# Head of a graph-network kernel: order of the loads, number and pace of the early tiles

## The chip, the cores and the metric

One core of a Trainium2 chip runs the kernel. The metric is the device time of one execution in microseconds (us), as the median of several runs.

## The reference

The input is a graph: `x` with 3125 nodes of 128 features, and 53125 edges (`src`, `dst`, a relation `type` of 0 to 7), sorted by `dst`, 17 to a node on average. Cut to what matters:

```python
h = relu(layernorm(x))
for L in 0, 1, 2:                                  # RGCN, W: [8, 128, 128]
    out = h @ root[L] + b[L]
    for r in range(8):
        msg = where(type == r, (h @ W[L][r])[src], 0)
        cnt = segment_sum(type == r, dst)
        out += segment_sum(msg, dst) / max(cnt, 1)
    h = relu(out)
x = x + h
g = relu(layernorm(x))                             # GIN
z = relu((g + segment_sum(g[src], dst)) @ W1 + b1) @ W2 + b2
out = x + g + (z - mean(z)) * rsqrt(var(z) + eps) * gamma + beta
```

## The kernel before

**Tiles.** Edges lie in 416 tiles of 128; nodes in 25 blocks of 128, loaded and normalized in 7 groups of 4 blocks (the last has one). For each layer there is an h table in DRAM, with one row for each node and relation (`h @ W[r]`). For each tile GpSimd gathers 128 rows of that table by an indirect DMA (`gather`, L1034) into a ring of 32 slots, VectorE builds a 128 x 64 selection matrix with the weights 1/count (`select`, L796), and TensorE multiplies both and so sums the tile into its window of 64 nodes (`sum_tile`, L464). GpSimd waits on `s_mm`, which counts batches of eight summed tiles, before it overwrites a slot: behind the first table, gather n (from 0, n a multiple of 8 and at least 32) waits until tile n - 25 of the count is summed. Layer 3 (GIN) works with a dense adjacency and no gathers.

**The early tiles.** The first 40 tiles of layer 0 (`FORE`) don't use the h table. GpSimd gathers their rows from the table of normalized x (`x0_table`, L1041), which is ready sooner. VectorE's `fore_select` (L767, 128 x 512, a ring of 12) keeps node and relation apart, `fore_tile` (L482) sums them into "key banks" of 64 nodes x 8 relations, ScalarE copies a full bank to SBUF, and `key_bank` (L492) multiplies it by the eight weights into the first sum. `fore_tile` opens a bank with a multiplication by zeros (L478). TensorE does 12 early tiles and then, by `head_order`, one tile of the h table and one early tile by turns.

**The head in order.** SP loads x (L947), then small weights, and stores each normalized group as x0 (L953). ScalarE issues `dst`, `type`, `src`, the first layer's relation weights (w0), and four loads of `dst` shifted by one and by 64 edges (L1066 to L1069; the first of them has 127 rows and 206.9 KB). Then it normalizes the groups (L598), turns them (`scalar_xT`, L592) and evacuates the 50 half blocks of the first table that TensorE makes (`transform`, L438; `evacuate`, L614). The tables go through a ring of three stages (`STAGES`) and out by SP (`store_rows`, L912 and L914). VectorE waits for all five `dst` loads (`s_edges`, L1173), builds keys, and tests by the shifted edges whether the graph fits the windows. TensorE sums the test (`s_metric` to `s_total`, L1391), and VectorE sets `flag` (L1211). Each engine reads the flag and branches into the windowed path (taken here) or a general one. SP waits for the flag before the first table store, GpSimd before the first x0 gather.

**Counts.** The keys of the edges are written to DRAM (L970 to L974) and come back broadcast to all partitions in chunks of 16 tiles (`load_chunk`, L923, 1088 KB each, two buffers). VectorE matches each tile's keys against them (L775) to count. SP puts chunks 0 and 1 in front of the table stores, and chunks 2 and 3 behind the stores of tables 10 and 19 (`CHUNK_BEHIND`).

**The order of TensorE in the table stage** is: per group the transforms of its blocks, then the turn of a later group; the sum of the test stands behind group 0.

Of the kernel before, what the change touches and what calls it, by code (L numbers as in the profile page):

```python
# [5 lines left out]
ALU = mybir.AluOpType  # L6
# [49 lines left out]
FORE = 40  # L56
FORE_RING = 12
KEY_BANK = 64
# [16 lines left out]
def gnn_kernel(nc, x, src_t, dst_t, type_t, limits, w_rel, root_w, bias_w,  # L75
# [16 lines left out]
    SLACK = max(P * t // DEG - LEAD - start_of[t] for t in range(TILES))  # L92
# [50 lines left out]
    FORE_STEP = start_of[BATCH] - start_of[0]  # L143
    assert all(start_of[t] == FORE_STEP * (t // BATCH) + STEP * (t % BATCH) - LEAD for t in range(FORE))

    def key_pieces(t):

        s, found = start_of[t], []
# [6 lines left out]
    KEY_BANKS = cdiv(start_of[FORE - 1] + SPAN, KEY_BANK)  # L155
# [18 lines left out]
    with ExitStack() as ctx:  # L174
# [59 lines left out]
        key_turn = shared(4 * P).rearrange("p (q k) -> p q k", k=P)  # L234
# [4 lines left out]
        fore_at = shared(FORE).bitcast(I32)  # L239
        key_near = shared(FORE)  # L240
# [3 lines left out]
        fore_sel = early[:, taken[7]:taken[7] + FORE_RING * KEYS].rearrange("p (a k) -> p a k", k=KEYS)  # L244
        assert taken[8] - taken[7] == EARLY + NP and taken[9] - taken[7] >= FORE_RING * KEYS
# [11 lines left out]

        match = agg_s[:].rearrange("p a k -> p (a k)").bitcast(BF16).rearrange("p (a k) -> p a k", a=BATCH)
# [27 lines left out]
        s_edges = sem("s_edges")  # L286
        s_src = sem("s_src")
# [646 lines left out]
        CHUNK_BEHIND = {10: 2, 19: 3}  # L934
# [6 lines left out]
        def _(sp):  # L941
# [16 lines left out]
            for L in range(GIN):  # L958
                if L:
                    sp.dma_start(w_all[:, L, 0:REL, :], w_rel[L].rearrange("r f o -> f r o")).then_inc(s_w, 16)  # L960
                sp.dma_start(w_all[:, L, REL, :], root_w[L]).then_inc(s_w, 16)
                sp.dma_start(vecs[:, L:L + 1], bias_w[L].rearrange("(p o) -> p o", o=1)).then_inc(s_w, 16)
                store_x0(L)
            sp.dma_start(w_gin[:, 0, :], gin_w1).then_inc(s_w, 16)
            sp.dma_start(w_gin[:, 1, :], gin_w2).then_inc(s_w, 16)
            for n, v in enumerate((gin_b1, gin_b2, gamma, beta)):
                sp.dma_start(vecs[:, 3 + n:4 + n], v.rearrange("(p o) -> p o", o=1)).then_inc(s_w, 16)
# [7 lines left out]
            for g in range(GIN, GROUPS):  # L975
                store_x0(g)
            sp.wait_ge(s_key_out, 48)
            load_chunk(sp, 0)
            load_chunk(sp, 1)
            sp.wait_ge(s_flag, 1)  # L980
            fast = sp.value_load(flag[0:1, 0:1], min_val=0, max_val=1)
            with sp.If(fast != 0):
# [12 lines left out]
                for b in range(BLOCKS):  # L995
                    if turn_of(0, b, 1) >= CHUNK * (CHUNKS - 3):
                        store_rows(sp, 1, b)
                for b in range(BLOCKS):
                    store_rows(sp, 2, b)
            with sp.Else():  # L1000
                for b in range(BLOCKS):
                    store_rows(sp, 0, b)
                for c in range(2, CHUNKS):
# [16 lines left out]
        def _(pool):  # L1020
# [6 lines left out]
            nc.gpsimd.iota(iota_i, pattern=[[1, EARLY + NP]], base=-EARLY, channel_multiplier=0).then_inc(s_pool_const, 1)  # L1027
            pool.wait_ge(s_idx, 1)
# [8 lines left out]
            with pool.If(fast != 0):  # L1037
                pool.wait_ge(s_src, 32)
                pool.wait_ge(s_x0, 16 * GROUPS)
                for t in range(FORE):  # L1040
                    pool.indirect_dma_start(fore_rows[:, t, :], None, x0_table,  # L1041
                                            bass.IndirectOffsetOnAxis(ap=src_i[:, t:t + 1], axis=0)
                                            ).then_inc(s_fore_row[t // BATCH], 16)
# [17 lines left out]
        def _(act):  # L1061
# [24 lines left out]
            scalar_norm(act, GROUPS - 1)  # L1086
            for g in range(GROUPS):
# [8 lines left out]
            act.wait_ge(s_w, 16 * (2 * GIN + 2 + 6))  # L1096
# [66 lines left out]
        def _(dve):  # L1163
# [8 lines left out]
            dve.wait_ge(s_edges, 80)  # L1172
            nc.vector.tensor_scalar(dst_pad, dst_i3[:], 0.0, float(PAD_NODE + 1), ALU.is_lt, ALU.mult  # L1173
# [4 lines left out]
            nc.vector.tensor_tensor(dst_f3[:], dst_i3[:], dst_pad, ALU.add).then_inc(s_edge_f, 1)  # L1178
# [8 lines left out]
            dst, after, far = (dst_f3[:, n, 0:TILES] for n in range(3))  # L1187
            nc.vector.tensor_tensor(broke[:, 0, :], after, dst, ALU.is_lt)
# [23 lines left out]
            dve.wait_ge(s_iota, 1)  # L1212
            dve.wait_ge(s_flag, 1)
            fast = dve.value_load(flag[0:1, 0:1], min_val=0, max_val=1)
            with dve.If(fast != 0):
# [11 lines left out]
                match_to(BATCH)  # L1227
# [4 lines left out]
                for t in range(FORE, HEAD + SELS - BATCH, BATCH):  # L1232
# [3 lines left out]
                    for f in range(FORE_RING + t - FORE, min(FORE_RING + t - FORE + BATCH, FORE)):  # L1236
                        fore_select(dve, f)
# [60 lines left out]
            with dve.Else():  # L1298
                nc.vector.memset(norm[:], 0.0).then_inc(g_found, 1)
# [66 lines left out]
        def _(pe):  # L1366
# [26 lines left out]
            pe.wait_ge(s_w, 16 * (2 * GIN + 2 + 6))  # L1393
# [139 lines left out]
```

## Time and profile before

| | us |
|---|---|
| median of 3 runs | 1685.67 |
| lowest, highest | 1683.42, 1686.53 |
| profiled execution | 1682.43 |
| its span, first to last instruction | 1680.6 |

| engine | busy us | share of the span |
|---|---|---|
| GpSimd (POOL) | 1186.0 | 71% |
| TensorE (PE) | 1170.9 | 70% |
| VectorE (DVE) | 868.2 | 52% |
| ScalarE (ACT) | 645.3 | 38% |

Busy shares are means over stages with different limits. In the rows, SPq, ACTq and POOLq are the instructions by which an engine issues DMAs, and a name behind "<-" in brackets is what ended the idle time before the row. Line numbers are those of the kernel.

### The profile page before, as it was taken

Reading aid. Unit: us, or ns where it says so; the run is one execution under the profiler, and the core shown is the slowest. Engines: PE = TensorE matmul, PEld = TensorE weight load, DVE = VectorE, ACT = ScalarE, POOL = GpSimd, SP = SyncE. Lnnn points to the kernel's source line nnn. Section 1 sums busy time; section 2 is a strip of 40 time slices with the busy share of each in tenths; the row PEclk is TensorE's granted clock in tenths of the full one; section 3 lists DMA queues with packets and bytes.
Section 4 is the critical chain, followed back from the end, with each engine's and each line's share of the span. In section 5 each row is a group of like instructions: output and inputs, shape, how many; then the busy total and the mean of one; then the engine's idle time right before and its main releaser. Section 6 shows DMA issues by size and latency. Waiting matters only on the chain.

```text
span 1680.6 us, 17006 instructions
## 1 busy us (share of the span) xinstructions
PE 1170.9 (70%) x4448; PEld 775.0 (46%) x4448; DVE 868.2 (52%) x3241; ACT 645.3 (38%) x1137; POOL 1186.0 (71%) x1256
## 2 busy tenths in 40 slices
PE   3799565657566777777777878765667666666777
PEld 1357444435344544444454545544545454544543
DVE  4647855455555177787778777751222222222213
ACT  4520500000000278888888888860011111212224
POOL 0757777777777577777777777757777777777770
PEclk9899755555555555758575756575567776768898
DMA  6963544353533311323232323231111111111111
GB/s 169 314 231 106 184 130 134 123 162 100 164 116 93 100 54 54 96 60 97 59 98 59 98 59 97 67 98 52 53 52 53 52 54 52 53 52 53 53 53 40
DMA packets 81154, 159.35 MB, mean 95 GB/s; under 512 B 24337, under 2 KB 38556, under 8 KB 77724
## 3 DMA queue, kind: packets, MB, share of 16 engines
q0 software_dynamic: 39936, 81.87, 18.4%
q1 hardware_dynamic: 39354, 74.73, 12.5%
q10 hardware_dynamic: 1762, 1.59, 0.4%
q8 instruction: 39, 0.64, 0.2%
q14 instruction: 63, 0.52, 0.1%
HBM read 115.33 MB, written 42.77 MB: 94 GB/s over the span
## 4 chain that ended last, share of the span: by engine, by line
POOL 67%; issue 22%; PE 5%; DMA 3%; ACT 1%; ACTq 1%; DVE 1%; SPq 0%; POOLq 0%; DVEq 0%
POOL rows L1034 67%; PE ps_h L438 3%; DMA h_table<-stage 2%; DMA rows<-h_table,idx 1%; PE ps_agg L464 1%; DMA early<-in_dst_t 1%; ACTq L1067 1%; ACT early L598 0%; PE ps_agg L1483 0%; ACT stage L614 0%; PE ps_h L558 0%; PE ps_agg L541 0%; PE ps_a L558 0%; PE ps_a L564 0%; PE ps_h L529 0%
## 5 line engine op out<-in xcount | busy, mean ns | idle before, releaser
L1034 POOL DMA_INDIRECT rows<-h_table,idx x1208 | 1143.5, 947 | 398.5 <-issue 367.2
L464 PE MATMUL ps_agg<-sel,rows 128*128 128x64 f32 (+12 forms) x2786 | 718.8, 375 | 443.5 <-DMA rows<-h_table,idx 433.1
L464 PEld LDWEIGHTS ps_agg<-sel,rows 128*128 128x128 f32 x2786 | 605.3, 278 | 737.8 <-DMA rows<-h_table,idx 586.3
L796 DVE TENSOR_SCALAR sel<-iota,early,norm 128x64 f32<-128x64 f32 x1208 | 358.0, 329 | 435.4 <-PE ps_agg L464 433.6
L891 DVE TENSOR_TENSOR early<-ps_a,early 128x300 f32 x416 | 197.8, 475 | 126.2 <-PE ps_a L509 115.4
L702 ACT ACTIVATE scratch<-scratch,ones 128x300 bf16<-128x300 f32 x416 | 223.2, 536 | 50.4 <-PE ps_a L509 42.6
L708 ACT ACTIVATE scratch<-iota,code_lo 128x300 f32<-128x300 f32 x416 | 226.4, 545 | 12.5
L438 PE MATMUL ps_h<-w_all,xT 128*128 128x512 f32 x300 | 197.8, 772 | 16.7 <-ACT stage L614 16.7
L775 DVE TENSOR_SCALAR_CACHE_REDUCE agg_s<-scratch,key_f 128x256 bf16<-128x256 f32 x416 | 194.2, 472 | 27.1 <-DMA scratch<-key_rows 16.7
L509 PE MATMUL ps_a<-scratch 128*128 128x300 bf16 x416 | 169.7, 409 | 0.9 <-DVE early L891 0.9
L880 DVE TENSOR_SCALAR scratch<-iota,code_lo 128x128 bf16<-128x128 f32 x416 | 145.1, 349 | 0.0
L614 ACT COPY stage<-ps_h 128x512 f32<-128x512 f32 x100 | 57.6, 585 | 197.3 <-PE ps_h L438 176.1
L674 ACT CAST stage<-early 128x3072 bf16<-128x3072 uint8 x13 | 35.7, 2751 | 175.9 <-PE ps_a L529 172.7
L619 ACT ACTIVATE xT<-ps_agg,vecs 128x512 f32<-128x512 f32 (+2 forms) x16 | 9.4, 587 | 229.7 <-PE ps_agg L464 229.7
L509 PEld LDWEIGHTS ps_a<-scratch 128*128 128x128 bf16 x416 | 96.4, 232 | 1.8 <-issue 1.7
L438 PEld LDWEIGHTS ps_h<-w_all,xT 128*128 128x128 f32 x300 | 63.1, 243 | 45.4 <-ACT stage L614 22.5
L614 DVE COPY stage<-ps_h 128x512 f32<-128x512 f32 x50 | 34.1, 683 | 90.8 <-PE ps_h L438 90.8
L1041 POOL DMA_INDIRECT early<-x_table,early x40 | 38.2, 956 | 51.1 <-issue 51.1
L674 ACT CAST w_all<-early 128x3072 bf16<-128x3072 uint8 x12 | 32.9, 2751 | 74.4 <-PE ps_a L529 74.4
L626 ACT ACTIVATE hid<-ps_agg,vecs 128x512 f32<-128x512 f32 (+3 forms) x10 | 5.3, 526 | 135.3 <-PE ps_agg L464 135.3
L447 PE MATMUL ps_agg<-xT,w_all 128*128 128x512 f32 (+3 forms) x52 | 36.6, 801 | 10.7 <-issue 6.1
L482 PE MATMUL ps_a<-early 128*128 128x464 f32 (+29 forms) x150 | 42.1, 410 | 0.0
(128 smaller groups left out, 546.0 us busy)
## 6 DMA issues: line engine op xcount, KB each, us to landing
h_table<-stage SPq DMA_DIRECT2D x150, 256.0 KB, 2.5
scratch<-key_rows SPq DMA_DIRECT2D x26, 1088.0 KB, 6.1
rows<-h_table,idx POOLq DMA_INDIRECT x1208, 2.5
x_rows<-in_x SPq DMA_DIRECT2D x6, 256.0 KB, 7.1
x_table<-early SPq DMA_DIRECT2D x6, 256.0 KB, 3.0
out<-early SPq DMA_DIRECT2D x6, 256.0 KB
w_all<-in_W SPq DMA_DIRECT2D x2, 512.0 KB, 4.2
early<-x_table,early POOLq DMA_INDIRECT x40, 4.0
```

The source lines that it names most:

```text
L438: nc.tensor.matmul(half_bank(L, b, half)[:], xT[:, block_of(b)], w_all[:, L, 4 * half:4 * half + 4, :].rearrange("p r o -> p (r o)"), star ...
L464: mm = nc.tensor.matmul(sums_of(L, k)[:, at:at + width], rows[:, G % SLOTS, :], sel[:, G % SELS, in_window:in_window + width], start=False ...
L509: nc.tensor.matmul(ps_a[a % A_BANKS][:, 0:HOT], low[:, a % HOTS, :], hot[:, a % HOTS, :], start=True, stop=True).then_inc(s_step, 1)
L614: copy(stage[:, H % STAGES, 512 * half:512 * half + 512], half_bank(L, b, half)[:]).then_inc((s_evA, s_evD)[half], 1)
L674: nc.scalar.copy(fill_of(b), adjacency[:, b, 0:SPARE]).then_inc(s_fill, 1)
L702: nc.scalar.activation(hot[:, a % HOTS, :], apart[:, a % 2, :], ACT.Relu, bias=ones[:, 0:1], scale=-1.0).then_inc(s_hot, 1)
L708: nc.scalar.activation(apart[:, a % 2, :], iota[:, EARLY:EARLY + HOT], ACT.Abs, bias=code[:, a:a + 1]).then_inc(s_apart, 1)
L775: done = nc.vector.tensor_scalar(match[:, t % BATCH, :], chunks[:, c % 2, at:at + 2 * P], key_f[:, t:t + 1], 0.0, ALU.is_equal, ALU.add, a ...
L796: done = nc.vector.tensor_scalar(mine, here, dst, norm[:, t:t + 1], ALU.is_equal, ALU.mult)
L880: nc.vector.tensor_scalar(low[:, a % HOTS, :], iota[:, EARLY:EARLY + P], lo_f[:, a:a + 1], None, ALU.is_equal).then_inc(s_low, 1)
L891: nc.vector.tensor_tensor(mine, ps_a[a % A_BANKS][:, 0:HOT].rearrange("p (b d) -> p b d", d=REACH), mine, ALU.add).then_inc(s_add, 1)
L1034: pool.indirect_dma_start(rows[:, slot, :], None, table, bass.IndirectOffsetOnAxis(ap=column, axis=0)).then_inc(landed, 16)
```

## The change

SP: w0 is loaded behind x instead of by ScalarE; x0 stores 0 to 4 come before the key store; root weights, biases and the other small loads (14) go two at a time behind the stores of tables 0 to 6. These seven tables are stored before SP waits for the flag. The relation weights of layers 1 and 2 (`load_w`) are loaded behind the last table store. Chunks 2 and 3 stand behind tables 13 and 20.

ScalarE: `dst`, `type` and `src` are loaded first, and the four shifted loads are issued behind all norms and the first `scalar_xT`, in front of the table's evacuations.

VectorE: pads and converts only the unshifted `dst` at first, and the shifted ones behind all groups of x, when it also waits for them (`s_shifted`). TensorE sums the test behind group 1.

GpSimd: the x0 gathers stand in front of the wait for the flag. `FORE` is 48, and the head has two early tiles to each later tile (`FORE_PACE`), so that it ends at tile 66 instead of 68. The early windows have their own starts (`fore_start`). Some buffers lie elsewhere.

```diff
-FORE = 40
+FORE = 48
 FORE_RING = 12
+FORE_PACE = 2
...
-    for t in range(FORE_RING, FORE):
-        head_order += [("tile", FORE + t - FORE_RING), ("fore", t)]
-    HEAD = 2 * FORE - FORE_RING
+    for t in range(FORE_RING, FORE, FORE_PACE):
+        head_order += [("tile", FORE + (t - FORE_RING) // FORE_PACE)] + [("fore", f) for f in range(t, t + FORE_PACE)]
+    HEAD = FORE + (FORE - FORE_RING) // FORE_PACE
...
+                    if b == 0 and L == 1:
+                        pe.wait_ge(s_wr, 16 * (GIN - 1))
...
-        CHUNK_BEHIND = {10: 2, 19: 3}
+        SP_BRANCH = 7
+        CHUNK_BEHIND = {13: 2, 20: 3}
...
-            for L in range(GIN):
-                if L:
-                    sp.dma_start(w_all[:, L, 0:REL, :], w_rel[L].rearrange("r f o -> f r o")).then_inc(s_w, 16)
...
+            sp.dma_start(w_all[:, 0, 0:REL, :], w_rel[0].rearrange("r f o -> f r o")).then_inc(s_w0, 16)
+            for g in range(5):
+                store_x0(g)
...
+            for b in range(SP_BRANCH):
+                store_rows(sp, 0, b)
+                for into, what in small_loads[2 * b:2 * b + 2]:
+                    sp.dma_start(into, what).then_inc(s_w, 16)
...
             sp.wait_ge(s_flag, 1)
...
-                for b in range(BLOCKS):
+                for b in range(SP_BRANCH, BLOCKS):
                     store_rows(sp, 0, b)
...
+                load_w()
...
+            pool.wait_ge(s_src, 32)
+            pool.wait_ge(s_x0, 16 * GROUPS)
+            for t in range(FORE):
+                pool.indirect_dma_start(fore_rows[:, t, :], None, x0_table,
+                                        bass.IndirectOffsetOnAxis(ap=src_i[:, t:t + 1], axis=0)
+                                        ).then_inc(s_fore_row[t // BATCH], 16)
             pool.wait_ge(s_idx, 1)
             pool.wait_ge(s_flag, 1)
...
-            act.dma_start(w_all[:, 0, 0:REL, :], w_rel[0].rearrange("r f o -> f r o")).then_inc(s_w0, 16)
-            act.dma_start(dst_i3[0:P - 1, 1, :], dst_t[1:P, 0:COLS]).then_inc(s_edges, 16)
...
             scalar_norm(act, GROUPS - 1)
+            scalar_xT(act, 0)
+            act.dma_start(dst_i3[0:P - 1, 1, :], dst_t[1:P, 0:COLS]).then_inc(s_shifted, 16)
+            act.dma_start(dst_i3[0:HALO, 2, :], dst_t[HALO:P, 0:COLS]).then_inc(s_shifted, 16)
+            act.dma_start(dst_i3[HALO:P, 2, :], dst_t[0:HALO, 1:COLS + 1]).then_inc(s_shifted, 16)
+            act.dma_start(dst_i3[P - 1:P, 1, :], dst_t[0:1, 1:COLS + 1]).then_inc(s_shifted, 16)
...
-            dve.wait_ge(s_edges, 80)
...
+            dve.wait_ge(s_edges, 16)
...
             norm_x(dve, GROUPS - 1)
...
+            dve.wait_ge(s_shifted, 64)
+            nc.vector.tensor_scalar(dst_pad[:, 1:3, :], dst_i3[:, 1:3, :], 0.0, float(PAD_NODE + 1), ALU.is_lt, ALU.mult
+                                    ).then_inc(s_edge_f, 1)
...
                 table0(g)
-                if g == 0:
+                if g == 1:
                     pe.wait_ge(s_metric, 1)
```

## Rows read from the trace of the kernel before

**Rows 1.** Page: chain that ended last by engine and line; costliest group

```profile
POOL 67%; issue 22%; PE 5%; DMA 3%; ACT 1%; ACTq 1%; DVE 1%; SPq 0%; POOLq 0%; DVEq 0%
...
L1034 POOL DMA_INDIRECT rows<-h_table,idx x1208 | 1143.5, 947 | 398.5 <-issue 367.2
```

**Rows 2.** Waits of GpSimd: who it waited for, us in total, times, longest

```profile
POOL rows L1034 <- issue: 367.2, 1205, 0.3
...
POOL rows L1034 <- DMA h_table<-stage: 31.3, 3, 11.8
```

**Rows 3.** Timeline, GpSimd: start us, us, line, operation, out<-in, count [idle before]

```profile
45.02 1.11 POOL L1041 DMA_INDIRECT early<-x_table,early  x1 [39.26 <-issue]
...
94.20 0.94 POOL L1041 DMA_INDIRECT early<-x_table,early  x1 [0.30 <-issue]
104.80 0.94 POOL L1034 DMA_INDIRECT rows<-h_table,idx  x1 [9.65 <-DMA h_table<-stage]
```

**Rows 4.** Timeline, TensorE in the head

```profile
104.81 3.12 PE L482 MATMUL ps_a<-early 128*128 128x296 f32 x8
...
123.46 0.33 PE L464 MATMUL ps_agg<-sel,rows 128*128 128x64 f32 x2
123.63 1.08 PE L482 MATMUL ps_a<-early 128*128 128x280 f32 x4
124.55 0.33 PE L464 MATMUL ps_agg<-sel,rows 128*128 128x64 f32 x2
...
158.88 5.89 PE L492 MATMUL ps_agg<-hid,w_all 128*128 128x64 f32 x48
164.59 2.58 PE L464 MATMUL ps_agg<-sel,rows 128*128 128x30 f32 x22
```

**Rows 5.** Timeline, all engines, 0 to 44

```profile
3.58 8.92 ACTq L1067 DMA_DIRECT2D early<-in_dst_t  x1
4.73 0.87 DVE L746 BATCH_NORM_STATS2 ln_stat<-x_rows 128x6 f32<-128x128 f32 x4 [2.97 <-DMA x_rows<-in_x]
...
23.31 0.81 DVE L1173 TENSOR_SCALAR rows<-early 128x1251 f32<-128x1251 int32 x1 [7.57 <-DMA early<-in_dst_t]
...
34.86 2.02 ACT L598 ACTIVATE early<-x_rows,ln_nm,ln_rs 128x128 f32<-128x128 f32 x5
...
35.27 0.59 DVE L1188 TENSOR_TENSOR rows<-early 128x416 f32<-128x416 f32 x1
...
37.25 1.54 ACT L614 COPY stage<-ps_h 128x512 f32<-128x512 f32 x3
...
37.91 1.26 SPq L923 DMA_DIRECT2D scratch<-key_rows  x2
...
43.03 0.16 DVE L1211 TENSOR_SCALAR flag<-ps_a 128x1 int32<-128x1 f32 x1 [0.60 <-PE ps_a L1391]
```

**Rows 6.** DMA issues: count, KB each, median us to landing (where known)

```profile
early<-in_src_t ACTq DMA_DIRECT2D x1, 208.5 KB, 5.2
...
early<-in_dst_t ACTq DMA_DIRECT2D x1, 206.9 KB
```

**Rows 7.** Windows: stretch, length, busy by engine, TensorE's clock, DMA share, GB/s

```profile
12.50:23.30 10.80, 1.08 (x4) 0.71 (x4) 0.34 (x2) 3.42 (x7) 0.00 (x0) 1.00 0.42 115
37.90:104.80 66.90, 52.66 (x117) 22.77 (x118) 36.21 (x147) 32.72 (x55) 38.24 (x41) 0.85 0.91 313
110.00:115.00 5.00, 5.00 (x24) 3.77 (x23) 4.02 (x14) 0.00 (x0) 3.78 (x5) 1.00 0.19 52
...
110.00:165.00 55.00, 55.00 (x313) 43.00 (x311) 43.19 (x174) 3.51 (x6) 41.90 (x44) 1.00 0.37 114
```

**Rows 8.** Timeline, SP's queue: store of table 7

```profile
58.23 0.32 SPq L912 DMA_DIRECT2D h_table<-stage  x1
```

**Rows 9.** Timeline, VectorE in the head: early selects

```profile
118.29 2.78 DVE L767 TENSOR_SCALAR early<-iota,early,norm 128x512 f32<-128x512 f32 x6
```

More of the change, by code:

```diff
@@ L91, in gnn_kernel @@
     start_of = [P * (t - t % BATCH) // DEG - LEAD + STEP * (t % BATCH) for t in range(TILES)]
-    SLACK = max(P * t // DEG - LEAD - start_of[t] for t in range(TILES))
+    FORE_STEP = start_of[BATCH] - start_of[0]
+    fore_start = [FORE_STEP * (t // BATCH) + STEP * (t % BATCH) - LEAD for t in range(FORE)]
+    assert all(fore_start[t] <= start_of[t] for t in range(FORE))
+    SLACK = max(P * t // DEG - LEAD - s for t, s in [*enumerate(start_of), *enumerate(fore_start)])
     assert all(P * t // DEG - LEAD >= start_of[t] >= -EARLY for t in range(TILES)) and SLACK < LEAD
@@ L142, in gnn_kernel @@
     assert FORE % BATCH == 0
-    FORE_STEP = start_of[BATCH] - start_of[0]
-    assert all(start_of[t] == FORE_STEP * (t // BATCH) + STEP * (t % BATCH) - LEAD for t in range(FORE))
     def key_pieces(t):
-        s, found = start_of[t], []
+        s, found = fore_start[t], []
         for j in range(KEY_BANKS):
@@ L153, in key_pieces @@
         return found
-    KEY_BANKS = cdiv(start_of[FORE - 1] + SPAN, KEY_BANK)
+    KEY_BANKS = cdiv(fore_start[FORE - 1] + SPAN, KEY_BANK)
     key_tiles = [[t for t in range(FORE) if any(p[0] == j for p in key_pieces(t))] for j in range(KEY_BANKS)]
@@ L238, in gnn_kernel @@
         fore_rows = shared(FORE * D).rearrange("p (a f) -> p a f", f=D)
-        fore_at = shared(FORE).bitcast(I32)
-        key_near = shared(FORE)
+        fore_at = rest[:, 0:FORE].bitcast(I32)
+        key_near = rest[:, FORE:2 * FORE]
         assert taken[-1] <= OWN + BLOCKS * NA // 4
@@ L243, in gnn_kernel @@
         KEYS = REL * KEY_BANK
-        fore_sel = early[:, taken[7]:taken[7] + FORE_RING * KEYS].rearrange("p (a k) -> p a k", k=KEYS)
-        assert taken[8] - taken[7] == EARLY + NP and taken[9] - taken[7] >= FORE_RING * KEYS
+        fore_sel = early[:, taken[6]:taken[6] + FORE_RING * KEYS].rearrange("p (a k) -> p a k", k=KEYS)
+        assert taken[7] - taken[6] == EARLY + NP and taken[8] - taken[6] >= FORE_RING * KEYS
         y_rows = xr_rows
@@ L256, in gnn_kernel @@
         base_i = key_f[:, 0:TILES].bitcast(I32)
+        key_turn = agg_s[:, 0, :].rearrange("p (q k) -> p q k", k=P)
         match = agg_s[:].rearrange("p a k -> p (a k)").bitcast(BF16).rearrange("p (a k) -> p a k", a=BATCH)
@@ L286, in gnn_kernel @@
         s_edges = sem("s_edges")
+        s_shifted = sem("s_shifted")
+        s_wr = sem("s_wr")
         s_src = sem("s_src")
@@ L957, in _ @@
                 load_x(g)
-            for L in range(GIN):
-                if L:
-                    sp.dma_start(w_all[:, L, 0:REL, :], w_rel[L].rearrange("r f o -> f r o")).then_inc(s_w, 16)
[L961 to L967, printed above, removed]
+            sp.dma_start(w_all[:, 0, 0:REL, :], w_rel[0].rearrange("r f o -> f r o")).then_inc(s_w0, 16)
+            for g in range(5):
+                store_x0(g)
             whole = COLS // P
@@ L974, in _ @@
             sp.dma_start(key_rows[0:1, 0:HALO], halo[:]).then_inc(s_key_out, 16)
-            for g in range(GIN, GROUPS):
+            for g in range(5, GROUPS):
                 store_x0(g)
@@ L979, in _, with load_w @@
             load_chunk(sp, 1)
+            small_loads = [(w_all[:, L, REL, :], root_w[L]) for L in range(GIN)]
+            small_loads += [(vecs[:, L:L + 1], bias_w[L].rearrange("(p o) -> p o", o=1)) for L in range(GIN)]
+            small_loads += [(w_gin[:, 0, :], gin_w1), (w_gin[:, 1, :], gin_w2)]
+            small_loads += [(vecs[:, 3 + n:4 + n], v.rearrange("(p o) -> p o", o=1))
+                            for n, v in enumerate((gin_b1, gin_b2, gamma, beta))]
+            for b in range(SP_BRANCH):
+                store_rows(sp, 0, b)
+                for into, what in small_loads[2 * b:2 * b + 2]:
+                    sp.dma_start(into, what).then_inc(s_w, 16)
+            assert 2 * SP_BRANCH >= len(small_loads)
             sp.wait_ge(s_flag, 1)
             fast = sp.value_load(flag[0:1, 0:1], min_val=0, max_val=1)
+            def load_w():
+                for L in range(1, GIN):
+                    sp.dma_start(w_all[:, L, 0:REL, :], w_rel[L].rearrange("r f o -> f r o")).then_inc(s_wr, 16)
             with sp.If(fast != 0):
-                for b in range(BLOCKS):
+                for b in range(SP_BRANCH, BLOCKS):
                     store_rows(sp, 0, b)
@@ L1000, in _ @@
             with sp.Else():
-                for b in range(BLOCKS):
+                for b in range(SP_BRANCH, BLOCKS):
                     store_rows(sp, 0, b)
+                load_w()
                 for c in range(2, CHUNKS):
@@ L1037, in _ @@
             with pool.If(fast != 0):
[L1038 to L1043, printed above, removed]
                 for L in range(GIN):
@@ L1072, in _ @@
             scalar_norm(act, 0)
-            scalar_sd(act, 2)
-            scalar_norm(act, 1)
-            scalar_xT(act, 0)
             whole = COLS // P
-            for g in range(3, GROUPS):
+            for g in range(2, GROUPS):
                 scalar_sd(act, g)
                 scalar_norm(act, g - 1)
-                if g == 4:
+                if g == 5:
                     act.wait_ge(s_key_turn, 1)
@@ L1092, in _ @@
                     evacuate(act, nc.scalar.copy, 0, b, 1)
-                if g == 0:
+                if g == 2:
                     act.wait_ge(s_pool_const, 4)
                     nc.scalar.copy(iota[:], iota_i).then_inc(s_iota, 1)
-            act.wait_ge(s_w, 16 * (2 * GIN + 2 + 6))
+            act.wait_ge(s_w, 16 * (GIN + GIN + 2 + 4))
             act.wait_ge(s_flag, 1)
@@ L1171, in _ @@
             norm_x(dve, 0)
-            dve.wait_ge(s_edges, 80)
-            nc.vector.tensor_scalar(dst_pad, dst_i3[:], 0.0, float(PAD_NODE + 1), ALU.is_lt, ALU.mult
+            dve.wait_ge(s_edges, 16)
+            nc.vector.tensor_scalar(dst_pad[:, 0, :], dst_i3[:, 0, :], 0.0, float(PAD_NODE + 1), ALU.is_lt, ALU.mult
                                     ).then_inc(s_edge_f, 1)
@@ L1177, in _ @@
             dve.wait_ge(s_edge_f, 1)
-            nc.vector.tensor_tensor(dst_f3[:], dst_i3[:], dst_pad, ALU.add).then_inc(s_edge_f, 1)
+            nc.vector.tensor_tensor(dst_f, dst_i3[:, 0, :], dst_pad[:, 0, :], ALU.add).then_inc(s_edge_f, 1)
             dve.wait_ge(s_src, 32)
@@ L1187, in _ @@
             dst, after, far = (dst_f3[:, n, 0:TILES] for n in range(3))
+            dve.wait_ge(s_shifted, 64)
+            nc.vector.tensor_scalar(dst_pad[:, 1:3, :], dst_i3[:, 1:3, :], 0.0, float(PAD_NODE + 1), ALU.is_lt, ALU.mult
+                                    ).then_inc(s_edge_f, 1)
+            dve.wait_ge(s_edge_f, 4)
+            nc.vector.tensor_tensor(dst_f3[:, 1:3, :], dst_i3[:, 1:3, :], dst_pad[:, 1:3, :], ALU.add
+                                    ).then_inc(s_edge_f, 1)
+            dve.wait_ge(s_edge_f, 5)
             nc.vector.tensor_tensor(broke[:, 0, :], after, dst, ALU.is_lt)
@@ L1225, in match_to @@
                             norm_batch(dve, m // BATCH)
-                match_to(BATCH)
+                match_to(min(CHUNK * 2, FORE + BATCH))
+                dve.wait_ge(s_iota, 1)
                 for t in range(FORE_RING):
@@ L1235, in _ @@
                         match_to(s + BATCH + 1)
-                    for f in range(FORE_RING + t - FORE, min(FORE_RING + t - FORE + BATCH, FORE)):
+                    for f in range(FORE_RING + FORE_PACE * (t - FORE), min(FORE_RING + FORE_PACE * (t - FORE + BATCH), FORE)):
                         fore_select(dve, f)
@@ L1298, in _ @@
             with dve.Else():
+                dve.wait_ge(s_iota, 1)
                 nc.vector.memset(norm[:], 0.0).then_inc(g_found, 1)
@@ L1392, in _ @@
                                      ).then_inc(s_total, 1)
-            pe.wait_ge(s_w, 16 * (2 * GIN + 2 + 6))
+            pe.wait_ge(s_w, 16 * (GIN + GIN + 2 + 4))
             pe.wait_ge(s_key_copy, 2)
```

6 lines of the change are left out of this document (removed).

## The prediction

> **What bounds the kernel now.** I read the chain of waits first: GpSimd's gathers fill two thirds of it and "issue" most of the rest; the line groups show that the issue time is GpSimd's own, between two gathers [rows 1]. A gather and the gap behind it take (1143.5 + 367.2) / 1208 = 1.25 us. In the waits of GpSimd nothing stands but issue and three waits for a finished h table, at the layers' starts [rows 2]: it never waits for a free slot. So time falls only if GpSimd issues fewer gathers behind the first table, or the first table is finished sooner. The timeline shows the 40 x0 gathers from 45.02 to 95.1 and the first gather from the h table at T0 = 104.80 [rows 3]. So T0 is set by the table, not by the x0 gathers. I split the change into what it does before T0 and after it. The profiled execution took 1682.43 us (span 1680.6, 1.8 outside it), 3.2 less than the median of the runs, 1685.67; I sum against the former and carry the difference to the latter.
>
> **Fewer gathers.** L0 issues 368 gathers behind the table instead of 376: 8 x 1.25 = -10.0 us. The 48 x0 gathers take 48 x 1.25 = 60 us. They stand in front of the branch now and wait only for x0 and src. If x0 is stored by about 25 (below), they end at 85, and the table hides them as long as T0 is later than that.
>
> **The ring of row slots.** This is the wait that the change can create. Behind T0, TensorE does the early tiles, two to each later tile. In the timeline of TensorE a later tile costs 0.17 (123.46 to 123.63), an early tile 0.92 (123.63 to 124.55), and three key banks behind each other 5.7, or 1.9 each (158.88 to 164.59) [rows 4]; opening a bank is two 512-wide matmuls like an early tile's work, 0.92. Check on before, from the first early tile at 104.81: 40 x 0.92 + 5 openings x 0.92 (bank 0 is open already) + 6 banks x 1.9 + 28 tiles x 0.17 + about 2.1 for opening the second sum and for tiles on two sums = 59.7; the trace has 59.8 [rows 4]. After: the last early window ends at node 386 instead of 326, so there are seven key banks of 64 nodes instead of six. Until tile 71 is summed: 48 x 0.92 + 6 x 0.92 + 7 x 1.9 + 24 x 0.17 + 2.4 = 69.4 us behind T0. GpSimd needs tile 71 (the third batch of eight) before its 49th gather, which it would reach at 48 x 1.25 = 60.0. So it waits: +9.4 us. Before, the third batch (tile 63) was far ahead: there are 28 tiles in the head, and each has one early tile before it. An early tile 0.06 us cheaper or dearer moves this by 3 us: +6 to +13. VectorE's share hides: of the 22 us that eight tiles and 16 early ones take TensorE, its 16 early selects take 7.4 (six in 2.78) [rows 9], and 14 stay for eight selects and matches. The gain of 10.0 is thus nearly paid back: sum behind T0 -0.6.
>
> **x first.** Before, the issue of ScalarE's second shifted load was stuck from 3.58 to 12.5, VectorE had statistics from 4.73 but stood until 23.31 for the shifted edges, the last normalization began at 34.86 and the first evacuation at 37.25 [rows 5]. In the change nothing stands in front of the norms but dst, type and src, of which src landed in 5.2 us [rows 6]. From a first norm at about 8 (statistics at 4.73 and two groups of them) with 1.9 us a group (five norms in 2.02, and a square root) [rows 5] they end at about 21; with xT and four issues (some 3 us) evacuation starts at about 25, 12 us sooner, and the first two chunk loads go out at about 22.3 instead of 37.91 [rows 5]. w0 moves to SP behind x: it has 10 us to spare until xT. By itself this would move T0 by up to 15.6 us.
>
> **What takes its place: the flag.** Now the shifted edges are loaded from about 22, while chunks, tables and gathers move, and the flag waits for them. The row to read is the 127-row load. A 128-row load of the same size, 208.5 KB, landed in 5.2 us beside x [rows 6]. The shifted ones were awaited until 23.31, and from 12.5, when ScalarE's blocked issue came through, to 23.3 the DMA engines moved only 115 GB/s at a share of 0.42 [rows 5, 7]. 206.9 KB in 10.8 us is 19.2 GB/s, a sixteenth of the 313 GB/s that all engines move in the table stage [rows 7]. I read this as one DMA engine with all 127 rows. The Trainium skill, "DMA: Bandwidth & Descriptors", section "Why a DMA increments its semaphore by 16 and not by 1", says that a DMA from SP or ACT is split over the largest number up to 16 that divides its rows, one for 127; by it the 10.8 us hold again wherever this load is put, and the trace agrees (19.2 GB/s).
>
> In its new place that DMA engine also has the SP queue's chunks and tables and GpSimd's gathers. With equal turns 10.8 us of work need twice that and, with a third queue at times, about 30: landed at 51. From the shifted edges to the flag there are pads and sums (some 1.6) and then, as before, what went from 35.27 to 43.19, 7.9: flag at about 61, against 43.19 [rows 5]. Queued behind it: on TensorE the total stands behind table group 1, so tables 8 to 24 wait; SP stores tables 0 to 6 and then waits; VectorE's matches; ScalarE's evacuations through the ring of three. From table 7's store to T0 before took 104.80 - 58.23 = 46.6 us, with two chunk loads in it [rows 8] as after; the x0 gathers end 10 us sooner relative to it (-2), and the iota copy is now in this stretch. So T0 = 61.3 + 45 = 106, or +1.5.
>
> A second way to it: from the chunk issue to T0 the engines were busy 0.91 x 66.9 = 60.9 us, idle 6.0 [rows 7]. After: less three x0 stores (-2), 8 more gathers at 0.19 x 1.25 = 0.24 each (+1.9) [rows 7], 14 small loads (+2), and 10.8 on the one engine on which every store also waits: 73.6 + 6 = 79.6, T0 = 22.3 + 79.6 = 102. That is the floor if the flag comes early. The roof: if ScalarE's queue gets a third of the turns, the load lands at 60, flag 69.5, T0 115. So T0 moves by -3 to +10. The Trainium skill, same page, section "Queues, rings and completion order", has each DMA engine take turns between queues by packets; by that the flag would lie inside this range, and no row here shows the turns.
>
> The two later weight loads move behind the last table store; the edge that waits for them (the second layer's tables) comes 60 us later, and the next chunk is needed some 15 us behind T0: nothing. Chunk loads behind tables 13 and 20 instead of 10 and 19, the removed iota wait and the new overlays: nothing, since T0 goes by the sum of transfers. If T0 were under 85, the x0 gathers would end last instead.
>
> Sum: 1682.4 - 10.0 + 9.4 + 1.5 = 1683.3; by the median, 1685.67 + 0.9 = 1686.6.
>
> **Rivals.** *The shifted loads are quick* (the 10.8 us was something else, such as ScalarE's blocked queue): landed at 28, flag 40, T0 = 22.3 + 60.9 + 1.9 + 6 = 91, moves -14; with -0.6 this gives 1671. For it: the trace shows no single DMA engine. Against: the 19.2 GB/s. *No ring wait*: TensorE gains on GpSimd, for instance because it begins the early tiles before T0; 1685.7 - 10 + 1.5 = 1677. Against it: before it began them at T0 exactly [rows 3, 4], and its own sum fits. *The flag comes still later* (slower): the load gets a third of the turns beside chunks and tables; T0 +10, time 1695. It decides from a landing later than about 55, where tables 7 to 24 with their 46.6 us start after 64.5. For it: every chunk row is larger than an edge row. *TensorE's clock falls in the head* (slower): it was 1.00 (2.4 GHz) from 110 to 165, fully busy [rows 7], and the head now lasts 70 us of the same work; from a loss of 4 us on it is slower, a quarter at 1.2 GHz would cost 17, 1703. *The gathers in front of the branch bring nothing by themselves*: that is part of my forecast, since the table ends last.
>
> **Numbers.** Forecast (one engine, flag near 61, ring wait 6 to 13, T0 -3 to +5), 1679 to 1693: 0.50, of it 0.07 faster, 0.31 same, 0.12 slower. Shifted loads quick, 1671: 0.22, faster. No ring wait, 1677: 0.09, faster. Flag much later, 1695: 0.13, slower. Clock, 1703: 0.04, slower. The rest 0.02, same. A measurement of this kernel tells about 0.2% (3.4 us) from no change. Faster 0.38, same 0.33, slower 0.29. The range takes in the quick loads and the late flag, 1670 to 1696; the forecast's own is 1679 to 1693.
>
> **What would show it.** 48 x0 gathers from about 25, done by 86. The flag instruction near 61 (40 if the loads are quick, 70 if late) and SP idle in front of it between the stores of tables 6 and 7. First gather from the table at 103 to 110. GpSimd waiting for TensorE before gathers 41 and 49 behind T0, 6 to 13 us together. TensorE's mean granted clock 1.00 in the head, its early tiles done about 68 us behind T0. The prediction is wrong if the flag comes before 50 or if the ring wait is missing.

## The result and the profile after

The changed kernel took 1672.95 us (median of 4 runs, 1670.15 to 1676.15) against 1686.1 before; the ratio is 0.9924, with a 95% interval of 0.9897 to 0.9951. It is 13 us faster, where the forecast was 1686.6, no change. Two later series, on two chips, gave 0.9938 (0.9925 to 0.9950) and 0.9950 (0.9937 to 0.9962), so 8 to 13 us in all. The profiled execution took 1675.47, with a span of 1673.4, 7.2 shorter than before's.

The page's chain after:

```profile
POOL 64%; issue 21%; PE 8%; DMA 4%; DVE 1%; ACT 1%; SPq 0%; ACTq 0%; POOLq 0%; DVEq 0%
...
L1057 POOL DMA_INDIRECT rows<-h_table,idx x1200 | 1139.3, 949 | 401.1 <-issue 364.3
```

The second line answers to the gathers of [rows 1]: 1200 instead of 1208, at (1139.3 + 364.3) / 1200 = 1.25 us as before. The waits of GpSimd, against [rows 2]:

```profile
POOL rows L1057 <- issue: 364.3, 1195, 0.3
POOL rows L1057 <- DMA h_table<-stage: 28.9, 3, 10.9
...
POOL rows L1057 <- PE ps_agg L470: 7.9, 2, 6.8
```

The third is new: the wait for a free row slot. Its two places, and the ends of the x0 gathers, stand in GpSimd's timeline, against [rows 3]:

```profile
29.85 1.11 POOL L1048 DMA_INDIRECT early<-x_table,early  x1 [24.07 <-DMA x_table<-early]
...
90.28 0.94 POOL L1048 DMA_INDIRECT early<-x_table,early  x1 [0.30 <-issue]
98.94 0.94 POOL L1057 DMA_INDIRECT rows<-h_table,idx  x1 [7.72 <-DMA h_table<-stage]
...
150.92 0.95 POOL L1057 DMA_INDIRECT rows<-h_table,idx  x1 [1.08 <-PE ps_agg L470]
...
167.47 0.95 POOL L1057 DMA_INDIRECT rows<-h_table,idx  x1 [6.85 <-PE ps_agg L470]
```

T0, the first gather behind the first table, came at 98.94 instead of 104.80. The sum is -5.9 for T0, -10.0 for eight gathers, +7.9 for the ring: -8.0, and the span shows -7.2. The head, all engines, against [rows 5]:

```profile
19.03 0.49 ACTq L1097 DMA_DIRECT2D early<-in_dst_t  x1
...
19.55 4.59 ACTq L1098 DMA_DIRECT2D early<-in_dst_t  x1
...
25.23 0.81 SPq L929 DMA_DIRECT2D scratch<-key_rows  x2
...
25.80 1.57 ACT L620 COPY stage<-ps_h 128x512 f32<-128x512 f32 x3
...
39.27 1.07 ACT L620 COPY stage<-ps_h 128x512 f32<-128x512 f32 x2 [9.36 <-DMA h_table<-stage]
...
41.63 0.59 DVE L1203 TENSOR_SCALAR rows<-early 128x834 f32<-128x834 int32 x1 [22.65 <-DMA early<-in_dst_t]
...
50.64 0.15 DVE L1232 TENSOR_SCALAR flag<-ps_a 128x1 int32<-128x1 f32 x1
...
51.72 0.32 SPq L918 DMA_DIRECT2D h_table<-stage  x1
```

The 127-row load is issued at 19.03 and the shifted edges are awaited until 41.63. Beside it the ring of three table stages stands still for 9.36 us: table 0, stored from 26.42, hasn't landed until 39.3. The flag comes at 50.64, and table 7's first store at 51.72. Before the chunk issue at 25.23, SP waits for the key store to land (SP's waits):

```profile
SPq L929 <- DMA key_rows<-halo: 4.0, 1, 4.0
```

In windows (columns as in [rows 7]): from the load's issue to the chunk issue, from there to the load's landing, from the chunk issue to T0, and in the head behind T0:

```profile
19.03:25.20 6.17, 4.16 (x5) 1.83 (x6) 0.00 (x0) 1.96 (x5) 0.00 (x0) 1.00 0.46 139
25.20:41.60 16.40, 8.46 (x20) 3.42 (x19) 0.00 (x0) 5.38 (x10) 9.01 (x10) 0.82 0.86 309
...
25.20:98.90 73.70, 59.52 (x151) 27.19 (x150) 41.01 (x159) 33.43 (x57) 47.05 (x48) 0.91 0.85 293
...
110.00:165.00 55.00, 55.00 (x306) 42.58 (x304) 38.57 (x148) 3.52 (x6) 37.95 (x40) 0.99 0.30 90
```

From the chunk issue to T0 the DMA share fell to 0.85 from 0.91, although more stood in the queues. That 15 engines wait for one is my reading, since no view shows single engines; the runs below bear it out, with a share of 0.89 and 0.90 over the same stretch once the load is split (a_split, a_split_2) and 0.78 once it is doubled (a_twice). TensorE's clock was 0.99 on average in the head.

Before, TensorE's first early tile and T0 fell together ([rows 4], 104.81). After, the first early tile is this (TensorE's timeline):

```profile
90.60 2.72 PE L488 MATMUL ps_a<-early 128*128 128x296 f32 x8
```

It began 8.3 us ahead of T0.

### The profile page after: what moved, and what is told of

Read it like the earlier page. It is cut to its first block, busy times and chain, and to the rows that moved or that the text cites. A ratio compares the mean times of both kernels' runs of the same rounds, so it can differ in the third digit from the quotient of the medians.

```text
span 1673.4 us, 17085 instructions
## 1 busy us (share of the span) xinstructions
PE 1186.4 (71%) x4482; PEld 787.1 (47%) x4482; DVE 873.2 (52%) x3243; ACT 647.0 (39%) x1138; POOL 1190.5 (71%) x1256
## 4 chain that ended last, share of the span: by engine, by line
POOL 64%; issue 21%; PE 8%; DMA 4%; DVE 1%; ACT 1%; SPq 0%; ACTq 0%; POOLq 0%; DVEq 0%
POOL rows L1057 64%; PE ps_a L488 2%; PE ps_h L444 2%; DMA h_table<-stage 2%; PE ps_agg L470 1%; DMA early<-in_dst_t 1%; DMA rows<-h_table,idx 1%; PE ps_agg L498 1%; DMA x_rows<-in_x 0%; ACT early L604 0%; PE ps_a L484 0%; ACT stage L620 0%; PE ps_agg L1505 0%; PE ps_h L564 0%; PE ps_a L564 0%
## 5 line engine op out<-in xcount | busy, mean ns | idle before, releaser
L1057 POOL DMA_INDIRECT rows<-h_table,idx x1200 | 1139.3, 949 | 401.1 <-issue 364.3
L470 PE MATMUL ps_agg<-sel,rows 128*128 128x64 f32 (+13 forms) x2770 | 719.0, 378 | 432.7 <-DMA rows<-h_table,idx 419.8
L444 PEld LDWEIGHTS ps_h<-w_all,xT 128*128 128x128 f32 x300 | 64.1, 246 | 49.9 <-issue 21.2
L1048 POOL DMA_INDIRECT early<-x_table,early x48 | 47.1, 980 | 38.4 <-DMA x_table<-early 24.1
L488 PE MATMUL ps_a<-early 128*128 128x464 f32 (+38 forms) x182 | 49.1, 410 | 0.0
L453 PE MATMUL ps_agg<-xT,w_all 128*128 128x512 f32 (+3 forms) x52 | 36.2, 794 | 11.3 <-issue 6.1
```

The costliest lines, as they stand in the source:

```text
L470: mm = nc.tensor.matmul(sums_of(L, k)[:, at:at + width], rows[:, G % SLOTS, :], sel[:, G % SELS, in_window:in_window + width], start=False ...
L488: mm = nc.tensor.matmul(ps_a[j % A_BANKS][:, at:at + width], fore_rows[:, t, :], fore_sel[:, t % FORE_RING, in_window:in_window + width], ...
L1057: pool.indirect_dma_start(rows[:, slot, :], None, table, bass.IndirectOffsetOnAxis(ap=column, axis=0)).then_inc(landed, 16)
```

## The experiments

Labels with `a_` edit the changed kernel, those with `b_` the kernel before. A ratio is against before, measured on the same chip, with its 95% interval; T0, flag, landing and ring wait are read from each trace as above. Four of the kernels first ran on a chip on which the kernel before itself took 2031 us (in b_split's trace there GpSimd waited 109.6 us for TensorE and 90.9 for tables); their ratios there (b_fore48 1.0107, b_split 0.9964, a_wlate 1.0022, a_pe24 1.0044) say nothing of the usual chip, and I ran them again under the label `_2`.

### The changed kernel, unedited

> The changed kernel again, unedited, to see how its time spreads on one chip beside the edited ones. Before: first gather behind the first table (T0) at 104.8 us, changed: 98.9, two waits of GpSimd for TensorE of 7.9 us in sum. Either theory: about 1673 us, ratio to before 0.992, T0 97 to 101, ring wait 6 to 10 us.

> The changed kernel unedited on the same chip, so that its edited versions are set against it and not against before alone: ratio to before 0.992 to 0.995.

Measured: 1673.8 us, 0.9938 (0.9925 to 0.9950), T0 98.2, flag 50.0, ring wait 8.7. A second time 1674.28, 0.9950 (0.9937 to 0.9962), T0 97.8, flag 49.9, ring wait 10.0. These are the marks for the edits.

### Is it one DMA engine? The 127 rows in two loads

```diff
-act.dma_start(dst_i3[0:P - 1, 1, :], dst_t[1:P, 0:COLS]).then_inc(s_shifted, 16)
+act.dma_start(dst_i3[0:112, 1, :], dst_t[1:113, 0:COLS]).then_inc(s_shifted, 16)
+act.dma_start(dst_i3[112:P - 1, 1, :], dst_t[113:P, 0:COLS]).then_inc(s_shifted, 16)
...
-dve.wait_ge(s_shifted, 64)
+dve.wait_ge(s_shifted, 80)
```

> The 127-row shifted load is issued as two loads of 112 and 15 rows, nothing else. Theory A (the 127 rows go through one DMA engine, 10.8 us alone and 22.6 beside other queues, from 19.0 to 41.6, and this load sets the landing that ends the stall of the stage ring and the flag): the shifted edges land by about 30, the flag comes by 40 instead of 50.6, ScalarE's stall of 9.4 us before its seventh evacuation falls to about 3, T0 near 92 (-5 to -8), the time 5 to 8 us below the changed kernel. Theory B (the load is late because all queues share 16 full engines): landing, flag and T0 stay within 2 us of 41.6, 50.6 and 98.9.

> The changed kernel with only the split load again, beside the run with 40 early tiles, to set the two apart on one chip. If the 8 saved gathers are paid back by the ring wait (9.9 us in its trace): the same time within 2 us. If the earlier T0 leaves room: 3 us or more faster with 48.

Measured: 1668.46 us, 0.9908 (0.9893 to 0.9922), and again 1665.85, 0.9890 (0.9874 to 0.9907). Timeline of a_split:

```profile
18.95 0.75 ACTq L1098 DMA_DIRECT2D early<-in_dst_t  x1
...
26.34 0.60 DVE L1204 TENSOR_SCALAR rows<-early 128x834 f32<-128x834 int32 x1 [7.79 <-DMA early<-in_dst_t]
...
34.44 1.08 ACT L620 COPY stage<-ps_h 128x512 f32<-128x512 f32 x2 [6.20 <-DMA h_table<-stage]
...
44.84 0.16 DVE L1233 TENSOR_SCALAR flag<-ps_a 128x1 int32<-128x1 f32 x1 [9.35 <-PE ps_a L1414]
...
93.45 0.94 POOL L1057 DMA_INDIRECT rows<-h_table,idx  x1 [8.87 <-DMA h_table<-stage]
```

The same bytes are there at 26.34 instead of 41.63, ScalarE's second issue takes 0.75 instead of 4.59, and T0 is 5.5 sooner than in the first trace, 4.7 sooner than in a_same beside it (98.2). Theory A holds, B falls. The flag gains 5.8 only, not 11: its last 9.35 us are a wait for TensorE, on which the total stands behind the table's second group, and that group is held by the stage ring. The ring's stall fell to 6.20 and not to 3 as expected, so most of it isn't due to this load. SP's wait for the key store is nearly gone:

```profile
SPq L929 <- DMA key_rows<-halo: 0.7, 1, 0.7
```

So the load had held up this store too. The first chunks go out at 21.31 instead of a_same's 24.77, 3.5 us sooner, and from there to T0 it takes 72.1 instead of 73.4: the greater part of the gain lies ahead of the chunk issue. The Trainium skill, "DMA: Bandwidth & Descriptors", section "Why a DMA increments its semaphore by 16 and not by 1", gives 127 rows one engine, 112 rows 16 and 15 rows 15. The two traces agree, with 22.6 us against at most 7.8 from issue to use.

### The same load twice

```diff
+act.dma_start(rows_flat[0:P - 1, 3400:3400 + COLS].bitcast(I32), dst_t[1:P, 0:COLS]).then_inc(s_shifted, 16)
...
-dve.wait_ge(s_shifted, 64)
+dve.wait_ge(s_shifted, 80)
```

> The same 127 rows are loaded a second time, right behind the first, into a spare piece of SBUF, and the wait for the shifted edges counts it too; 207 KB more. Theory A (one engine): landing moves by 10 to 22 us, from 41.6 to 52 to 64, flag to 61 to 73, T0 by +8 to +15. Theory B (16 engines share it): 207 KB at 313 GB/s is 0.7 us, T0 within 2 us of 98.9.

Measured: 1680.0 us, 0.9985 (0.9976 to 0.9994), 6 slower than a_same beside it. Timeline:

```profile
18.99 4.67 ACTq L1098 DMA_DIRECT2D rows<-in_dst_t  x1
...
23.69 15.81 ACTq L1099 DMA_DIRECT2D early<-in_dst_t  x1
...
41.15 1.08 ACT L620 COPY stage<-ps_h 128x512 f32<-128x512 f32 x2
...
52.30 0.60 DVE L1204 TENSOR_SCALAR rows<-early 128x834 f32<-128x834 int32 x1 [33.88 <-DMA early<-in_dst_t]
...
109.35 0.96 POOL L1057 DMA_INDIRECT rows<-h_table,idx  x1 [18.72 <-DMA h_table<-stage]
```

207 KB more, 0.7 us at the rate of all engines, put the landing off by 11.3 us (a_same: 41.02) and T0 by 11.2, as theory A has it; its 11 us are the load's own 10.8 on one engine. The trace shows a second way in which such a load costs: the issue behind it blocks ScalarE for 15.81 us, and the first evacuation comes at 41.15. The time rose by 6.2, less than T0, and the ring wait fell by 4.8, to 3.9.

### The split in the kernel before

The same edit there, with `s_edges` and 96 instead of 80.

> The kernel before with only its 127-row load issued as 112 and 15 rows, once more, on a chip where the kernel before takes its usual 1680 to 1686 us (the first time it took 2031). Theory A: VectorE's wait for the shifted edges is gone (it ended at 23.3), flag at 34 to 36, T0 96 to 99, the time 6 to 9 us below before. Theory B: no change.

Measured: 1674.96 us, 0.9942 (0.9926 to 0.9959), 9.3 below before. Timeline:

```profile
3.50 1.14 ACTq L1067 DMA_DIRECT2D early<-in_dst_t  x1
...
13.17 0.81 DVE L1174 TENSOR_SCALAR rows<-early 128x1251 f32<-128x1251 int32 x1 [4.81 <-DMA early<-in_dst_t]
...
27.10 1.55 ACT L614 COPY stage<-ps_h 128x512 f32<-128x512 f32 x3
...
32.89 0.16 DVE L1212 TENSOR_SCALAR flag<-ps_a 128x1 int32<-128x1 f32 x1 [0.60 <-PE ps_a L1392]
...
96.07 0.99 POOL L1034 DMA_INDIRECT rows<-h_table,idx  x1 [10.98 <-DMA h_table<-stage]
```

Against [rows 5] the wait for the edges ends 10.1 us sooner (13.17 for 23.31), the flag 10.1, the first evacuation 10.2, T0 8.7. One load in two pieces gives the old kernel what the whole change gave it.

### The early tiles alone, and the head alone

b_fore48 takes the hunks of `FORE`, `FORE_PACE`, `fore_start` and the overlays into the kernel before, and nothing of the loads and their order. a_fore40 goes the other way:

```diff
-FORE = 48
+FORE = 40
...
-FORE_PACE = 2
+FORE_PACE = 1
```

> The kernel before with only the early-tile part of the change (48 early tiles, two between later tiles), once more, on a chip where before takes its usual time. Theory A: x0 gathers to 105, T0 105 to 106, ring wait 8 to 10, within 3 us of before. Rival: 8 to 10 us below before.

> The changed kernel with 40 early tiles and one between later tiles as before, so only the order of the head is changed. Theory A (the 8 gathers saved, 10.0 us, are nearly all paid back by the ring wait of 7.9): no ring wait, eight gathers more, T0 unchanged at 98 to 100, the time within 3 us of the changed kernel and 5 to 6 below the kernel before. Rival (the early tiles carry the gain): 8 to 10 us slower than the changed kernel, that is at the time of before.

> The changed kernel with both: the 127-row load as 112 and 15 rows, and 40 early tiles, one between later tiles. What the order of the head is worth once no load sits on one DMA engine. Theory A (the old head lost its time by that load alone): T0 within 3 us of the 96.1 that before with the split load has, time within 2 us of its 0.9942 of before, 1673 to 1676. Theory C (the order gives something of its own): T0 89 to 92, ratio 0.991 to 0.992, 1668 to 1671.

Measured: b_fore48_2 1683.46 us, 0.9990 (0.9980 to 0.9999), 0.8 below before. Its timeline:

```profile
104.44 0.94 POOL L1043 DMA_INDIRECT early<-x_table,early  x1 [0.30 <-DMA h_table<-stage]
107.22 1.08 POOL L1036 DMA_INDIRECT rows<-h_table,idx  x1 [1.84 <-DMA h_table<-stage]
...
174.46 0.95 POOL L1036 DMA_INDIRECT rows<-h_table,idx  x1 [6.34 <-PE ps_agg L466]
```

Ten us of gathers saved, 2.4 lost at T0, and 6.3 lost at the ring: -1.3, measured -0.8. The early tiles bring nothing by themselves. T0 is not late for want of GpSimd: the last x0 gather ends at 105.4, and GpSimd then waits 1.84 for the table. The ring wait is below the 8 to 10 that I expected, and TensorE had begun the early tiles at 104.62, 2.6 ahead of T0. a_fore40: 1675.29, 0.9952 (0.9939 to 0.9965), T0 95.9, no ring wait; 1.5 slower than a_same beside it. I had expected T0 to stay at 98 to 100. In three pairs T0 comes 2.3 to 2.9 us later with 48 early tiles than with 40 (a_same 98.2 and a_fore40 95.9; a_split_2 92.4 and a_split_fore40 89.5; b_fore48_2 107.2 and before 104.8): the eight x0 gathers are hidden on GpSimd, but the table lands later with them. The order of the head carries the gain. a_split_fore40: 1669.27, 0.9911 (0.9898 to 0.9925), T0 89.5. Theory A, that the load alone held the old head back, is thus too strong: with the load split, the new order is still 6.6 us sooner at T0 than the old (96.1) and its ratio 0.003 lower, some 5 us. It is sooner by the chunk issue (21.1 against 27.9 in b_split_2); from there to T0 both take the same, 68.4 and 68.2. The eight early tiles bring 3.4 us beside it by a_split_2 on the same chip, and 0.5 by the ratio of a_split.

### The weights of layers 1 and 2 later

```diff
-                load_w()
...
                     load_chunk(sp, c)
+                    if c == 5:
+                        load_w()
```

The changed kernel's first later tile, in TensorE's timeline:

```profile
105.80 0.66 PE L470 MATMUL ps_agg<-sel,rows 128*128 128x64 f32 x2 [4.28 <-DMA rows<-h_table,idx]
106.26 2.37 PE L488 MATMUL ps_a<-early 128*128 128x24 f32 x4
108.42 1.91 PE L484 MATMUL ps_a<-wide 128*128 128x512 f32 x2
```

TensorE had its first twelve early tiles done before the rows came: it stood for 4.28 us, and then an early tile took 2.16 and a bank opening 1.70, at a granted clock of 0.50 (106.2 to 110.1), where an early tile takes 0.92 in [rows 4] and the same opening 0.86 in a_wlate_2, both at 1.00. The clock had been 1.00 until the stand (98 to 102).

> The changed kernel with the relation weights of layers 1 and 2 behind the sixth key chunk, once more, on a chip where before takes its usual time. If that load delays the first later tile's rows (6.9 us): rows after about 4 us, ring wait 4 to 6 instead of 8 to 9, 2 to 4 us below the changed kernel's 0.993 to 0.994. If the chunks do it: within 1 us.

> The changed kernel with the split load and the late weight loads together. If both gains stand (5 to 8 us and 2 us): 1662 to 1665, ratio to before 0.987 to 0.989, no wait of TensorE for the first later tile over 2 us. If the ring wait, which goes by TensorE's sum of work, takes the second one back: the same as the split alone, 0.989 to 0.991.

Measured: a_wlate_2 1671.32 us, 0.9917 (0.9903 to 0.9931), where a_same had 0.9938 and 0.9950. In TensorE's timeline:

```profile
91.91 2.72 PE L488 MATMUL ps_a<-early 128*128 128x296 f32 x8
...
102.67 0.33 PE L470 MATMUL ps_agg<-sel,rows 128*128 128x64 f32 x2
```

The tile starts at 102.67 with no wait, 4.1 behind T0, and the ring wait is one of 2.58, less than the 4 to 6 expected. a_split_wlate: 1661.38 us (1659.76 to 1664.67), 0.9882 (0.9868 to 0.9897), T0 91.4, ring wait 1.43, 12.9 below the changed kernel on the same chip (a_same_2). The two add up, as expected (0.987 to 0.989), and this version beats both kernels: T0 is 6.4 sooner than in a_same_2 and the ring wait 8.6 shorter.

```profile
91.43 0.95 POOL L1058 DMA_INDIRECT rows<-h_table,idx  x1 [6.89 <-DMA h_table<-stage]
...
153.76 0.95 POOL L1058 DMA_INDIRECT rows<-h_table,idx  x1 [1.43 <-PE ps_agg L470]
```

### More early tiles in front

24 early tiles stand in front of the first later tile, ten of them between the last five table blocks on TensorE:

```diff
-    head_order = [("fore", t) for t in range(FORE_RING)]
-    for t in range(FORE_RING, FORE, FORE_PACE):
+    head_order = [("fore", t) for t in range(FORE_FIRST)]
+    for t in range(FORE_FIRST, FORE, FORE_PACE):
...
+                    for t in early_tiles[2 * (b - 4 * TABLE_BRANCH):2 * (b - 4 * TABLE_BRANCH) + 2]:
+                        fore_tile(pe, t)
```

> The changed kernel with 24 early tiles in front of the first later tile, the first ten between the last table blocks, once more, on a chip where before takes its usual time. Theory A: ring wait 0 to 1 instead of 8 to 9, T0 +0 to +3, the time 5 to 9 us below the changed kernel (ratio to before 0.988 to 0.991). Rival (the wait only moves): within 2 us of the changed kernel (0.993 to 0.995).

> The changed kernel with the 127-row load as 112 and 15 rows, 24 early tiles in front of the first later tile (ten of them between the last table blocks), and the relation weights of layers 1 and 2 behind the sixth key chunk. Theory A: the parts add up: T0 93 to 95, no ring wait, 12 to 16 us below the changed kernel, 1658 to 1663, ratio to before 0.984 to 0.988. Rival (the parts share one cause): no better than the split alone, 1668, 0.991.

Measured: a_pe24_2 1676.25 us, 0.9956 (0.9942 to 0.9970), T0 100.0, ring wait 5.3. a_all 1668.68, 0.9905 (0.9889 to 0.9922), T0 95.6, ring wait 5.3. My expectation failed. The head now ends at tile 60, so all early tiles and key banks stand in front of tile 63, which GpSimd needs eight gathers sooner than tile 71; the one wait is before the 41st gather. T0 is 2 us later; that the early tiles between the table's matmuls do this is argued, not shown. a_all has all three edits, and its ratio is 0.0023 (3.9 us) above that of a_split_wlate, which goes without this one.

## Why the prediction was wrong

**Right.** Eight gathers at 1.25 were the saving. The place of the ring wait (before the 41st and 49th gather) was foretold, and that it pays back the gathers (b_fore48_2). The 127-row load on one engine was the right reading of [rows 5, 7]. The x0 gathers came later than forecast (29.85 to 91.2, not 25 to 86), still ahead of T0. The rival of quick loads was wrong in its mechanism, though its time, 1671, was nearest to the measured one.

**Right by luck: the size of the ring wait.** It was forecast at 9.4 with bounds 6 to 13 and measured 7.9, 8.7 and 10.0. The forecast let TensorE begin the early tiles at T0. It began 8.3 us sooner (90.60), which is the condition of the rival of no ring wait, to which I gave 0.09; by the sum that leaves a wait of 1.1. Then TensorE stood for 4.28 us for the first rows, and from there to the end of the second later tile it took 2.6 us more than in a_wlate_2 (105.80 to 111.71 against 102.67 to 105.99), at the lower clock: 1.1 + 4.3 + 2.6 = 8.0. Where the stand is missing, the head start alone gives the wait: 9.4 - 6.7 = 2.7 in a_wlate_2 (measured 2.6), 9.4 - 7.8 = 1.6 in a_split_wlate (1.4), 9.4 - 5.2 = 4.2 in a_twice (3.9), 9.4 - 2.6 = 6.8 in b_fore48_2 (6.3). So the price of TensorE's work was right, its start was wrong, and the stand, which the prediction didn't have, hid that. The rival of the clock had the fall to half speed, though for 4 us and not for a quarter of the head.

**The step that failed: when the shifted edges land.** I put it at 51, with T0 at 106 (+1.5); they landed at 41.6, T0 at 98.9 (-5.9). The two steps behind it held: landing to flag 9.0 (forecast 9.5), and table 7's first store, at 51.72 in the trace after, to T0 47.2 (forecast 45, before 46.6). What was mis-sized is the load's start and its company. The issue came at 19.03 and not at about 22, behind the norms and xT: ScalarE's DMA issues ran beside its last normalizations. The chunks came at 25.23 and not 22.3, since the wait for the key store held SP for 4.0 us. In the 6.2 us between the two the DMA engines were busy 0.46 on average, against 0.86 in the 16.4 us behind them. So the load had less company at its start than I gave it, and needed 22.6 in all where I had said 30; how much of its 10.8 was done by 25.23 no view shows. I had taken three queues in equal turns over the whole time. The flag, at 50.6, 50.0 and 49.9 in the three traces, lies at the bound of 50 that I had named as a sign of being wrong, and T0 is outside the 103 to 110 that I had named.

The second way in the prediction, by the engines' busy time, named 102 as the floor; the truth was 98.9, 73.7 behind the chunk issue where 79.6 was worked out. Its busy time was right (62.8 without the load, measured 0.85 x 73.7 = 62.6). The term that failed is the load: put in with all of its 10.8 on top of an idle 6.0, where the idle was 11.1 in all. Set against runs with the load split, it costs 1.3 to 3.5 us from the chunk issue to T0 (73.4 in a_same and 72.1 in a_split; 71.9 in a_fore40 and 68.4 in a_split_fore40), and 2.9 to 3.9 more ahead of it, by the later chunk issue.

**The choice between the two ways.** I let the flag decide T0 because it came last by my times. In the trace SP waits 2.3 us for it. The stage ring's stall of 9.36 us, by which table 0's stores hold up TensorE and ScalarE, begins sooner; 6.20 of it stay in a_split without the load. Over the changed heads, a_all aside, T0 is 46.4 to 49.8 behind the flag (flags from 42.1 to 61.3), but the ring's stall moves with it; in a_twice, where it is only 2.09, T0 is 48.0 behind the flag, but there ScalarE itself was blocked. Counted from the chunk issue instead, T0 comes 68.4 to 75.1 later in them, a_twice (84.6) aside, and 66.9 to 69.1 in the versions of the kernel before (b_split on the slow chip left out), in which the flag is 62 to 64 ahead of T0. No run parts these, so which of them sets T0 stays open.

**The time.** By the profile the change gave 7.2 us and by the medians 8.2 to 13.2; the profiled execution was 2.5 over its median and before's 3.7 under its own. The terms that the traces show sum to -8.0, which the two later series bear out and the first, with four runs on a side, exceeds. The wide range of 1670 to 1696 held the time, through its rivals' ends and not through the forecast's own 1679 to 1693; the forecast's sign was wrong, and by the summed chances faster (0.38) stood only just ahead of same (0.33).

## What to carry to other kernels

Look at the row count of every DMA in the head before moving it: here a load of 127 rows ran at a sixteenth of the rate, delayed a store beside it by some 3 us, and blocked the engine that issued the next one. Split such a load first; here two lines gave 9 us, as much as the rearranged head, and the rearrangement gave some 5 of its own on top.

Count the gathers saved against the work that takes their place behind the same wait: eight gathers of 1.25 us were paid back by eight early tiles and a key bank on TensorE through a ring of 32 slots. The bulk loads that nothing needs soon shouldn't stand in front of the first rows that a whole engine waits for. And when a forecast of a wait comes true, check where the work behind it began: here two errors cancelled.

## What the runs showed of the hardware

- A second DMA of the same 127 rows, 207 KB, put off the waiting reader by 11.3 us (a_twice), 18 GB/s, where 112 and 15 rows took at most 7.8 us together (a_split).
- The issue of a DMA behind it took 4.59 us (8.92 before, 15.81 in a_twice), and ScalarE's next copies stood behind it.
- ScalarE's DMA issues at 19.03 ran while its normalizations went on until 20.5.
- With 1 MB of weights and two key chunks issued just ahead of the first gathers, TensorE had the first rows 6.9 us behind the start of their gather; with the weights later, at most 4.1 (a_wlate_2).
- TensorE's granted clock was 1.00 until it stood for 4.28 us, and 0.50 for the 3.9 us behind (106.2 to 110.1); an early tile took 2.16 us there, 0.92 in [rows 4].
- The kernel before took 1682 to 1684 us on four chips and 2031 on one, where the table stage moved 184 GB/s at a DMA share of 0.55 (b_split's trace), against 313 at 0.91 in [rows 7].
